# A fused adaLN block on one core: the barrier between its halves removed, token shifts in copies and by DMA, a shorter inverse root, new instruction orders

## What is computed

```python
mod = (silu(c) @ wmod).reshape(8, 6, 1, 128)            # sa, ca, ga, sb, cb, gb; ga, gb kept away from 0
h = layernorm(x) * (1 + ca) + sa                        # x: (8, 256, 128), float32
x = x + ga * causal_attention(h)                        # 8 heads of 128, rope
h = layernorm(x) * (1 + cb) + sb
for i in range(6):                                      # "the stream"
    h = local_attention(shift_tokens(h), i) + h         # 16 heads of 64, windows of 32, q and k l2-normalised,
                                                        #   scaled, rotated
    h = ffn(shift_tokens(h), i) + h                     # layernorm, W1, a * gelu(gate), W2
x = x + gb * h

def shift_tokens(t):                                    # the second half of the channels moves one token on
    a, s = split(t, 2, -1); s = pad(s, 1 token)[:, :-1]
    return concatenate([a, s], -1)
```

## Time and profile before

| | |
|---|---|
| median of 3 runs | 1872.73 us (1865.93 to 1878.46) |
| the profiled execution's own time | 1868.75 us |
| its span, first to last instruction | 1867.0 us |
| mean granted clock of TensorE | 0.983 |
| busy: PE, weight loads, DVE, ACT, POOL | 93%, 77%, 79%, 75%, 79% |
| first attention up to the barrier | about 275 us |
| DMA queues, share of 16 engines | 11.8% the largest |

### The profile page before, as it was taken

How to read it: one execution, slowest core, us unless ns; L and a number is a source line. 1 busy time by engine, 2 the same in 40 slices (tenths; PEclk the granted TensorE clock), 3 DMA queues, 4 the chain that set the end, 5 groups by cost and what they waited for, 6 DMA issues and landing times. The chain is left out here.

```text
span 1867.0 us, 66200 instructions
## 1 busy us (share of the span) xinstructions
PE 1732.8 (93%) x26984; PEld 1428.9 (77%) x26985; DVE 1472.2 (79%) x2952; ACT 1404.0 (75%) x2772; POOL 1479.4 (79%) x1830
## 2 busy tenths in 40 slices
PE   6999967899999999999999999999999999999985
PEld 4788755777778888787887787877778877888773
DVE  5878847778977888888879787888888798889752
ACT  3777744678877888878877877888788878788862
POOL 3777757779888887988888879789888888898860
PEclk9999988999999999999999999999999999999998
DMA  4000011111121111111110211112111101110100
GB/s 140 1 1 1 1 36 34 31 44 32 31 68 44 33 43 32 58 44 42 44 32 22 68 44 43 31 33 67 40 37 44 32 22 41 38 50 22 37 27 23
DMA packets 45485, 70.67 MB, mean 38 GB/s; under 512 B 15476, under 2 KB 28928, under 8 KB 45184
## 3 DMA queue, kind: packets, MB, share of 16 engines
q1 hardware_dynamic: 43712, 64.34, 11.8%
q10 hardware_dynamic: 1472, 2.10, 0.3%
HBM read 21.33 MB, written 1.05 MB: 12 GB/s over the span
## 5 line engine op out<-in xcount | busy, mean ns | idle before, releaser
L1087 POOL TENSOR_TENSOR ra<-ra,rb 128x512 f32<-128x512 f32 x384 | 492.3, 1288 | 116.7 <-DVE rb L1083 111.6
L1132 POOL TENSOR_TENSOR qn<-ra,rs 128x512 f32<-128x512 f32 x384 | 401.3, 1058 | 7.2 <-POOL rs L1125 0.8
L1062 DVE TENSOR_REDUCE ss<-sq 128x8 f32<-128x512 f32 x384 | 260.4, 678 | 91.2 <-ACT sq L1051 91.2
L1214 POOL TENSOR_TENSOR sp<-sp,rl 128x512 f32<-128x512 f32 x192 | 200.0, 1046 | 61.7 <-DVE rl L1209 61.0
L1201 ACT ACTIVATE sp<-sp 128x512 f32<-128x512 f32 x192 | 121.7, 634 | 38.5 <-DVE sp L1196 38.1
L1205 DVE TENSOR_REDUCE sm<-sp 128x8 f32<-128x512 f32 x192 | 128.6, 670 | 15.5 <-ACT sp L1201 13.0
L1179 PE MATMUL pP<-kT,qT 64*32 64x64 f32 x4608 | 106.9, 226 | 2.8 <-issue 2.2
L1179 PEld LDWEIGHTS pP<-kT,qT 64*32 64x32 f32 x4608 | 93.8, 105 | 16.3 <-ACT kT L1152 11.0
L489 POOL TENSOR_TENSOR ra<-ra,rb 128x512 f32<-128x512 f32 x64 | 81.5, 1288 | 29.6 <-DVE rb L485 29.6
L1190 DVE TENSOR_REDUCE mx<-pS 128x8 f32<-128x512 f32 x48 | 32.9, 685 | 91.2 <-PE pP L1179 91.2
L1083 DVE TENSOR_TENSOR rb<-pQ,rope 128x512 f32<-128x512 f32 x144 | 97.9, 680 | 2.9 <-POOL ra L1087 2.9
(11 more groups left out here) (355 smaller groups left out, 6194.3 us busy)
## 6 DMA issues: line engine op xcount, KB each, us to landing
vs<-v SPq DMA_DIRECT2D x96, 384.0 KB, 3.3
wqkvA<-in_L_ffn_Wqkv SPq DMA_DIRECT2D x18, 512.0 KB, 5.6
vs<-v SPq DMA_DIRECT2D x96, 64.0 KB, 3.0
woB<-in_L_ffn_Wo SPq DMA_DIRECT2D x6, 512.0 KB, 4.2
w<-in_L_ffn_W SPq DMA_DIRECT2D x6, 341.0 KB, 2.9
out<-x SPq DMA_DIRECT2D x4, 256.0 KB, 2.3
x<-in_L_attn_x SPq DMA_DIRECT2D x1, 768.0 KB, 8.1
w<-in_L_ffn_W SPq DMA_DIRECT2D x12, 64.0 KB
```

What stands on the lines that cost most here:

```text
L1062: e.tensor_reduce(ss[:, j, :], sq[:, j % 2, :].rearrange("p (h d) -> p h d", d=DB), AX.X, ALU.add).then_inc(b_ss.sem, 1)
L1087: e.tensor_tensor(ra[:, j, :], ra[:, j, :], rb[:, j % 2, :], ALU.add).then_inc(b_ad.sem, 1)
L1132: e.tensor_tensor(qn[:, j % 4, :].rearrange("p (h d) -> p h d", d=DB), ra[:, j, :].rearrange("p (h d) -> p h d", d=DB), rs[:, c % 2, 8 * j ...
L1214: e.tensor_tensor(y, y, rl[:, u, :].unsqueeze(2).to_broadcast([P, 8, 64]), ALU.mult).then_inc(b_pn.sem, 1)
```

## The change

- *No barrier.* `barrier` and `mark_written` go. The tail of the first attention's last batch and the whole first pair of the stream are written out together in four new functions, `join_pe`, `join_act`, `join_dve`, `join_pool`; `stream` starts at the second pair. The memset of gT moves to its first use, `scaled_rope(0)` into batch 3.
- *Shifts in copies.* `xt_turn` is two plain transposes; `xt_high` and `xt_low` write lower and upper half apart, the upper one column on.
- *The FFN's shift by DMA.* `l_shift` is three DMAs on SP's queue, 112 rows, 15 rows, and one row that wraps; `l_first` moves to ACT and waits for them; `l_second` goes. SP's queue gets `l_shift` between the `move_values`.
- *Root in nine steps.* A start value, one residual and a polynomial: steps 0 to 4 on POOL, 5 to 8 on DVE.
- *Orders anew* in all four pair functions, with new bank tables. All turns of batch c + 1 now stand in the next pair.
- *Loads.* `load_ahead` moves from the layer's start to the place behind batch 3's `move_values`; layer 0's other weights are loaded at the start.
- *Finish* of quarters 0 to 2 moves into the last pairs and the remainder, right behind the pair function of DVE that ends the quarter.

```diff
-NORM = 12
-ROOM = (1024.0 / 27.0) ** 2
+EVEN = 112
+NORM, FIT = 9, 5
+SERIES = (1.0, -0.49999832, 0.37500061, -0.3139403, 0.27406215)
+ROOM = 1.0 / SERIES[4] ** 2
+HORNER = [x / SERIES[4] for x in SERIES[3::-1]]
...
         def xt_turn(e, l, c):
...
             for t in range(NT):
-                e.matmul(o[lo, t * P:(t + 1) * P], xc[:, t, lo], ident, start=True, stop=True)
-            e.matmul(o[hi, 0:P], xc[:, 0, hi], down, start=True, stop=True)
-            e.matmul(o[hi, P:T], xc[:, 1, hi], down, start=True, stop=False, skip_group_check=True)
-            e.matmul(o[hi, P:T], xc[:, 0, hi], wrap, start=False, stop=True, skip_group_check=True)\
-             .then_inc(b_xt.sem, 1)
+                i = flip(e, o, t, xr[:, (c % B) * NT + t, :])
+            i.then_inc(b_xt.sem, 1)
+
+        def shifted(l, c, x_):
+
+            o = xt_bank(l, c)
+            return ((x_[0:HALF, c % 2, :], o[0:HALF, 0:T]), (x_[HALF:M, c % 2, 1:T], o[HALF:M, 0:T - 1]))
 
         def xt_high(e, l, c):
...
-            e.copy(xsh[:, c % 2, :], banks[XT_BANK[c % 2]][:, 0:T]).then_inc(b_xh.sem, 1)
+            for dst, o in shifted(l, c, xsh):
+                i = e.copy(dst, o)
+            i.then_inc(b_xh.sem, 1)
...
+            for (dst, o), (h, _) in zip(shifted(l, c, xsl), shifted(l, c, xsh)):
+                i = e.tensor_tensor(dst, o, h.bitcast(F32), ALU.subtract)
+            i.then_inc(b_xs.sem, 1)
...
             elif n == 4:
-                e.tensor_scalar(p, t, -10.0 / 3.0, None, ALU.add).then_inc(b_rs.sem, 1)
...
+                e.tensor_scalar(t, t, -1.0, None, ALU.add).then_inc(b_rs.sem, 1)
+            elif n == FIT:
+                e.scalar_tensor_tensor(p, t, HORNER[0], t, ALU.add, ALU.mult).then_inc(b_rs.sem, 1)
+            elif n < NORM - 1:
+                e.scalar_tensor_tensor(p, p, HORNER[n - FIT], t, ALU.add, ALU.mult).then_inc(b_rs.sem, 1)
             else:
                 e.wait_ge(b_qn.sem, b_qn.at(it - 2, QK - 1))
-                e.tensor_tensor(rs[:, c % 2, :], t, y, ALU.mult).then_inc(b_rs.sem, 1)
+                e.scalar_tensor_tensor(rs[:, c % 2, :], p, HORNER[n - FIT], y, ALU.add, ALU.mult).then_inc(b_rs.sem, 1)
...
         def l_shift(e, l, q):
...
             e.wait_ge(b_wx.sem, b_wx.at(l * B + 2 * q + 1))
             e.sem_inc(e_hold.sem, 1)
             e.wait_ge(f_ln.sem, f_ln.at(it - 1))
             e.sem_inc(e_hold.sem, 1)
...
+            k = (q % FP) * FT
+            e.dma_start(fx[0:1, 1::NT, HALF:M], xr[P - 1:P, k:k + FT:NT, HALF:M]).then_inc(f_xs.sem, 16)
+            for lo, hi in ((EVEN, P - 1), (0, EVEN)):
+                e.dma_start(fx[lo + 1:hi + 1, :, :], xr[lo:hi, k:k + FT, :]).then_inc(f_xs.sem, 16)
+
+        def l_first(e, l, q):
             it = l * FP + q
...
+            e.wait_ge(b_wx.sem, b_wx.at(l * B + 2 * q + 1))
+            e.wait_ge(f_xs.sem, f_xs.at(it))
+            e.copy(fx[:, :, 0:HALF], xr[:, tiles(q), 0:HALF]).then_inc(f_xa.sem, 1)
...
-            barrier(e, 0)
-            mark_written(e)
+            join_pe(e)
             stream(e, pair_pe)
             remainder(e, pair_pe)
...
+                move_values(e, l, 2, 1)
+                l_shift(e, l, 0)
+                if l > 0:
+                    load_second(e, l)
+                move_values(e, l, 3, 0)
+                move_values(e, l, 3, 1)
                 if l < DEPTH - 1:
                     load_ahead(e, l + 1)
```

More of the change, by code:

```diff
@@ L1457, in pair_pe @@
             if on(p - 1):
-                e.wait_ge(b_ev.sem, b_ev.at(l * B + c - 1, 3))
-                turn_p(e, l, c - 1, 0)
-                e.wait_ge(b_oc.sem, b_oc.at(l * B + c - 2, 3))
+                scores(e, l, c - 1, 0)
+            if on(p):
+                e.wait_ge(b_ab.sem, b_ab.at(l * B + c, 0))
+            if on(p - 1) and not on(p) and not on(p):
+                e.wait_ge(b_oc.sem, b_oc.at(l * B + c - 2, 2))
+            if on(p - 1):
+                turn(e, l, c - 1, 5)
@@ L1464, in pair_pe @@
             if on(p - 1):
                 out_proj(e, l, c - 2, 0)
+            if on(p):
+                e.wait_ge(b_ab.sem, b_ab.at(l * B + c, 5))
+            if on(p - 1) and not on(p) and not on(p) and not on(p):
+                e.wait_ge(b_ev.sem, b_ev.at(l * B + c - 1, 0))
+            if on(p - 1):
+                turn_p(e, l, c - 1, 0)
                 scores(e, l, c - 1, 1)
@@ L1562, in pair_pe @@
             if on(p):
-                e.wait_ge(b_tc.sem, b_tc.at(l * B + c, 1))
-                proj(e, l, c + 1, 3)
+                scores(e, l, c, 0)
+                e.wait_ge(b_ab.sem, b_ab.at(l * B + c + 1, 2))
+                turn(e, l, c, 4)
+            if on(p - 1):
+                e.wait_ge(b_oc.sem, b_oc.at(l * B + c - 1, 2))
+            if on(p) and not on(p - 1):
+                e.wait_ge(b_tc.sem, b_tc.at(l * B + c, 2))
+            if on(p):
+                proj(e, l, c + 1, 4)
+                e.wait_ge(b_ev.sem, b_ev.at(l * B + c, 2))
+                proj(e, l, c + 1, 5)
+                e.wait_ge(b_tc.sem, b_tc.at(l * B + c, 4))
+                proj(e, l, c + 1, 6)
@@ L1587, in pair_pe @@
+            if on(p - 1) and not on(p):
+                e.wait_ge(b_oc.sem, b_oc.at(l * B + c - 1, 3))
             if on(p - 1):
                 out_proj(e, l, c - 1, 0)
+            if on(p):
+                scores(e, l, c, 1)
+                e.wait_ge(b_tc.sem, b_tc.at(l * B + c, 6))
+                turn_p(e, l, c, 0)
+            if on(p - 1):
                 out_proj(e, l, c - 1, 1)
             if on(p):
-                e.wait_ge(b_ab.sem, b_ab.at(l * B + c + 1, 5))
-                turn(e, l, c, 6)
@@ L2018, in pair_pool, with stream @@
                 normalise(e, l, c + 1, 2)
-                normalise(e, l, c + 1, 3)
-                soft_norm(e, l, c, 2)
-                soft_norm(e, l, c, 3)
-        def stream(e, pair):
-            for p in range(FP):
+                rotate_add(e, l, c + 1, 7)
+        def stream(e, pair, after=lambda p: None):
+            for p in range(1, FP):
                 pair(e, 0, p, lambda q: q >= 0)
```

1195 lines of the change are left out of this document (787 added, 408 removed).

## The result

The changed kernel takes 1849.97 us (median of 4 runs, 1844.50 to 1853.94), the kernel before 1871.17 beside it. The ratio is 0.989, with a 95% interval of 0.986 to 0.991. So it is faster by 21 us, in the range, but by less than half of the 54 us that I forecast. The profiled execution took 1852.71 us and has a span of 1850.9 us, 16.1 us less than before's 1867.0.

The account below looks back on a forecast made before the run. TensorE was taken to bind. Start 316, 23 pairs 1421.4, moved finish 3 and remainder 73 gave a span of 1813.4 us, against 1867.0; as a median of runs 1819 us, range 1770 to 1867.

Parts of the forecast that it names:

- What bounds the kernel: Whole stream: TensorE binds, busy 246.55 of 254.25 us a layer; the other three engines have 10 us or more spare per pair.
- together 2.05 us a pair leave the engine that binds, 47 us: xt_turn as two transposes saves TensorE 1.30 us a pair, l_shift's two matmul calls 0.75; over 23 pairs 47 us.
- The first rival: TensorE's busy time overstates it, so its 47 us buy nothing and only join and end remain: 1866 us; chance 0.08.
- Item 3: xt_high and xt_low as two 64-partition copies: 0.8 us a pair more on ACT and DVE each, hidden; effect on time zero.
- Item 4: FFN shift by three DMAs a pair: taken as covered at 3.3 + 0.4 us, 2.0 us late at 7.4; no wait at l_stats.
- Item 5: Root in nine steps: latency stays (4.6 against 4.5 us), POOL gains 1 us a batch, DVE's first step takes over 1 us.
- it fits, narrowly: VectorE's load per pair: 54.6 us of work and 3.9 held by POOL, 58.5 in 61.5.
- Item 6: New orders of the pair functions: 3 to 4 us of waits at a pair's head, net 0.3 added; pairs of 61.8 us.
- Item 7: Join without barrier: first projection near 270.5 us, DVE binds the first pair (some 44 us), second pair near 316 instead of 339.45.
- Item 8: Remainder after the last pair: all eight turns still to do, finish partly moved away; 73 us against 65.7.
- Item 9: Next projection weights loaded a pair and a half ahead of first use, some 90 us: costs nothing.

Follow-up runs that it names:

- b_keep: Kernel before without the shift's matmuls in xt_turn and l_shift, small matmuls keeping TensorE's instruction count: 1874.8 us, ratio 1.001 to the kernel before.
- b_out: Kernel before with the last three of eight head pairs in each out_proj call replaced by six small matmuls, as many instructions: 1870.1 us, ratio 1.001.
- a_out: Changed kernel with the last three of eight head pairs in each out_proj call replaced by six small matmuls: 1830.2 us, ratio 0.979 to the kernel before.

## Why the prediction was wrong, and where it was right

Forecast and measured, in the parts of the sum: 316 against 327.1 up to the second pair (+11.1); 1424.4 against 1449.2 for the 23 pairs (+24.8); 73 against 74.6 behind them (+1.6). Together 37.5 us, the distance from 1813.4 to 1850.9, which is most of the 53.6 us of span that I forecast as the gain. Of the pairs' 24.8 us, 14.8 are stalls at blocks' ends (33.1 in this stretch against 18.3), the other 10.0 longer pairs: 61.6 us each less stalls, where the forecast leaves 61.1 (and the kernel before had 62.8).

- *What bounds the kernel* was the step that failed, and with it the sum's largest term. "PE binds" rested on its busy time, and so "together 2.05 us a pair leave the engine that binds, 47 us" did. The matmuls went as sized, PE's busy time by 6.8 us a layer where I said 8. But in the old orders 26 to 38 us less of such work gains nothing (b_keep, b_out), and in the new ones 20 of 35 (a_out). The first rival, "PE isn't what binds", had this mechanism, at a chance of 0.08; its 1866 gave the orders nothing. The pairs less stalls, 61.6 us where the forecast leaves 61.1, come close by luck and not by the forecast's reason: putting 42 us of the work back costs 15, and the shift and the root by themselves lose in the old orders. That leaves the new orders as what gave most of the pairs' gain, which no run shows alone.
- *Item 3, the shift in copies*, is zero only in the new orders (0.23 us of wait at 329.64). In the old ones it is PE's wait for xt_low, up to 24 us.
- *Item 4, the DMA*, was right. VectorE waited for l_first once, in the remainder:

```profile
L1696 DVE BATCH_NORM_STATS2 fst<-fx x96: 273/276/296, 387.5 to 1825.3; 128x6 f32<-128x128 f32 x96
its engine sat idle before it (us, times) until:
  ACT fx L1689: 2.2, 1
```

- *Item 5, the root*: the first step over 1 us, the others 0.225, POOL idle 1 us before the first normalise, all as written. But "it fits, narrowly" costed it at nothing, and with rotate_add 6 behind POOL's steps it costs 12 us. Whether by VectorE's hold or by POOL's longer path from the sum to the normalise is open. VectorE wasn't full, as item 5 had it: it was busy 56.0 us of a pair's 63.3, hold included.
- *Item 6, the orders*: PE waits for qn as forecast, but 8.9 us in 16 pairs, under 0.6 a pair, where I had 3 to 4 with turn 6 (577.4 to 1590.9 us; us in total, times, longest):

```profile
PE pP L336 <- POOL qn L1513: 3.7, 4, 0.9
PE pS L336 <- POOL qn L1513: 2.7, 8, 0.5
PE pQ L336 <- POOL qn L1513: 2.0, 7, 0.4
PE pT L336 <- POOL qn L1513: 0.5, 3, 0.2
```

  All its idle time less the stalls grew from 18 to 30 us in 16 pairs, 0.8 a pair where I added 0.3. How the orders and the place of rotate_add 6 share the 10.0 us isn't shown.
- *Item 7, the join*: the first projection at 271.4 (270.5 forecast). VectorE is busy 45.0 of the 59 us from 268 to 327, my 44, but it waits for the other 14. I took one engine's sum for a chain of five. 2.0 of the 11.1 us are a stall at a block's end (at 312.6 us). The granted clock was 0.86 in these 59 us; what that cost no run shows.
- *Item 8* was right in its sum, 74.6 against 73, though no row gives the 3.3 us at its end; the rows leave 2.7 (1867.0 less 1858.84 less the 5.4 of finish).
- *Item 9, "Nothing"*: the load's place costs two stalls of over 4 us in four layers, where a block's end meets its loads; for the weights themselves "nothing" holds within 3 us.
- *Missing from the list*: the change takes 978 instructions from TensorE's program, and with them the places where blocks end. No sum of durations holds that. It is the 14.8 us in the pairs and the 2.0 in the join.

## What to carry to other kernels

An engine that is 97% busy in a hand-made order need not be the one that binds: take work away from it, with the same number of instructions, before counting on the gain. Number the instructions of a long unrolled program: stalls without a cause at the same number modulo 256 are blocks running dry, and a few instructions that do nothing, or a period of whole blocks, can be worth more than the work saved. Where POOL and VectorE both work from SBUF, try POOL's long instruction ahead of the short chain that VectorE ends, most of all where POOL waits there anyhow.

## What the hardware showed besides

- 64 idle instructions ahead of a program of 55,324 moved it by 4%. A fetched block takes 0.9 to 1.5 us, and TensorE goes on 1.2 to 1.6 us behind it. Mostly the fetch starts within 1.6 us of the block before it, at times 2 to 10 us after.
- A semaphore increment takes TensorE 0.15 us; a small bf16 matmul with its weight load 29 ns in a row on one group of the array, 11 ns spread over groups, and as long as a large one when it stands alone between matmuls of another type.
